# Causal attention scores by halves of 64 queries, in two 64-column tiles of TensorE

## The reference

```python
k = einsum('ihd,bpd->biph', W_K, x); q, v likewise
scores = einsum('biph,biqh->biqp', k, q)
masked = scores * tril - 1e10 * (1 - tril)
attn = softmax(masked / sqrt(128), axis=-1)
z = einsum('biqp,biph->biqh', attn, v)
out = einsum('df,bqf->bqd', W_O, z.reshape(b, q, 16 * 128))
```

## Time and profile before

| | |
|---|---|
| Runs: median (lowest to highest) of 3 | 977.67 us (977.49 to 978.47) |
| Profiled execution | 976.68 us |
| Its span, first to last instruction | 974.9 us |
| Mean granted TensorE clock | 0.995 of full |
| PE busy | 934.1 us, 96% |
| DVE, ACT, POOL busy | 627.8 us, 475.5 us, 239.0 us |
| DMA | 27.89 MB, mean 29 GB/s |

### The profile page before, as it was taken

The page is one execution under the profiler, slowest core; times in us unless marked ns, Lnnn a source line. Parts: engine busy times, 40 slices in busy tenths (PEclk is TensorE's granted clock), DMA queues, the critical chain, the costliest instruction groups (busy, mean ns, idle before and its releaser), DMA issues.

```text
span 974.9 us, 19976 instructions
## 1 busy us (share of the span) xinstructions
PE 934.1 (96%) x7621; PEld 793.7 (81%) x7621; DVE 627.8 (64%) x1383; ACT 475.5 (49%) x1593; POOL 239.0 (25%) x257
## 2 busy tenths in 40 slices
PE   7999999999999999999999999999999999999877
PEld 5777777899788888888888888888888887677657
DVE  6678887797875576564556454556456665777854
ACT  3877876444445554444344444434444554443431
POOL 3455786572011111111111010111111212110000
PEclk9999999999999999999999999999999999999989
DMA  8100000002330000000000000100010004000002
GB/s 304 38 2 3 2 2 2 2 1 90 108 152 1 1 1 2 1 1 2 1 1 2 1 1 1 44 18 1 1 58 30 1 1 176 1 2 2 2 1 87
DMA packets 10941, 27.89 MB, mean 29 GB/s; under 512 B 1824, under 2 KB 6976, under 8 KB 10208
## 3 DMA queue, kind: packets, MB, share of 16 engines
q1 hardware_dynamic: 10128, 26.41, 7.6%
q10 hardware_dynamic: 720, 0.20, 0.1%
HBM read 24.51 MB, written 2.10 MB: 27 GB/s over the span
## 4 chain that ended last, share of the span: by engine, by line
PE 84%; DVE 8%; ACT 4%; issue 2%; DMA 0%; POOL 0%; SPq 0%; DVEq 0%; ACTq 0%; POOLq 0%
PE bank L50 15%; PE bank L52 14%; PE bank L51 14%; PE bank L2035 6%; PE bank L1984 5%; PE bank L392 3%; PE bank L402 3%; PE bank L2025 3%; PE bank L1899 2%; PE bank L1908 2%; PE bank L414 2%; PE bank L1041 2%; PE bank L178 2%; PE bank L1031 2%; PE bank L1017 2%
## 5 line engine op out<-in xcount | busy, mean ns | idle before, releaser
L1845 POOL TENSOR_TENSOR wa_prob<-wa_prob,wa_rsum 128x512 f32<-128x512 f32 x64 | 67.5, 1055 | 405.2 <-DVE wa_rsum L2418 405.2
L2217 ACT ACTIVATE wa_prob<-wa_prob,wa_negmax 128x128 f32<-128x128 f32 x256 | 99.7, 390 | 66.3 <-DVE wa_negmax L2407 66.1
L50 PE MATMUL bank<-norm_xT_hi,wide_hi 128*128 128x512 f32 x256 | 106.0, 414 | 0.2 <-DVE norm_xT_lo L189 0.2
L51 PE MATMUL bank<-norm_xT_lo,wide_hi 128*128 128x512 f32 x256 | 101.0, 395 | 0.0
L52 PE MATMUL bank<-norm_xT_hi,wide_lo 128*128 128x512 f32 x256 | 101.0, 395 | 0.0
L2474 DVE TENSOR_TENSOR wa_z_lo<-bank,wa_z_hi 128x512 fp32r<-128x512 f32 x64 | 44.2, 691 | 86.9 <-ACT wa_z_hi L2251 86.4
L583 ACT ACTIVATE v_prob<-bank,la_negmax 128x128 f32<-128x128 f32 x256 | 91.1, 399 | 1.1 <-DVE la_negmax L661 1.1
L2225 ACT COPY wa_q<-bank 128x512 f32<-128x512 f32 x64 | 37.6, 587 | 93.6 <-PE bank L52 93.6
L2232 ACT COPY wa_v<-bank 128x512 f32<-128x512 f32 x64 | 37.3, 584 | 89.6 <-PE bank L52 89.6
L329 POOL TENSOR_TENSOR v_prob<-v_prob,la_rsum 128x512 f32<-128x512 f32 x64 | 66.5, 1041 | 51.8 <-DVE la_rsum L666 51.7
L173 POOL TENSOR_TENSOR norm_rstd<-norm_rstd,minus_half 128x4 f32<-128x4 f32 x23 | 24.6, 1069 | 206.1 <-DVE norm_rstd L133 175.2
(11 more groups left out here) (277 smaller groups left out, 2372.0 us busy)
## 6 DMA issues: line engine op xcount, KB each, us to landing
wide_raw<-in_wide_w SPq DMA_DIRECT2D x16, 512.0 KB, 6.8
em_w<-in_em_w SPq DMA_DIRECT2D x1, 4096.0 KB, 13.3
x<-in_x SPq DMA_DIRECT2D x4, 512.0 KB, 4.9
lc_kt<-in_ctx_rev SPq DMA_DIRECT2D x1, 2048.0 KB, 10.7
lc_toep<-in_toeplitz SPq DMA_DIRECT2D x1, 2048.0 KB, 14.5
li_kt<-in_ctx_rev SPq DMA_DIRECT2D x4, 512.0 KB, 6.6
out_x<-x SPq DMA_DIRECT2D x8, 256.0 KB, 2.9
w_or_y<-in_l_w SPq DMA_DIRECT2D x1, 1024.0 KB, 6.3
```

Source lines behind the costliest of these rows:

```text
L50: nc.tensor.matmul(out, a[0], b[0], start=start, stop=False, skip_group_check=True)
L51: nc.tensor.matmul(out, a[0], b[1], start=False, stop=False, skip_group_check=True)
L1845: nc.gpsimd.tensor_tensor(prob[:, s], prob[:, s], rsum[:, s, :].unsqueeze(2).to_broadcast([P, G, P]), ALU.mult).then_inc(prob_ok, 1)
L2217: last = nc.scalar.activation(prob[:, s, j, :], prob[:, s, j, :], ACT.Exp, bias=negmax[:, s, j:j + 1], scale=SCALE, accum_out=sums[:, s, j ...
```

## The change

Each batch's score matmul is replaced by two, each with 64 queries stationary. Their results go to partitions 0 to 63 (tile 0) and 64 to 127 (tile 1) of the bank. The first 64 queries take only the first 64 keys, except in steps 0 and 1, where they take all 128; the part that is then not written keeps finite scores of an earlier step, and the mask removes it. In even batches queries 0 to 63 are in tile 0, in odd ones in tile 1. For the odd batches the mask has its halves of rows exchanged, and the transposes of `turn` take a matrix with exchanged halves in place of the identity, which puts the queries back in order. The mask, the exchanged mask and the exchanged identity come in one load of 192 KB in place of 64 KB. The mask addition reads and writes the same elements as 2 x 256 in place of 4 x 128.

```diff
--- before.py
+++ after.py
@@ -1708,7 +1708,8 @@
         le_w, le_u = pr.le_w32, pr.le_u32
         v = sb("v", [P, 2, G, VH * HD])
         z = (sb("z_hi", [P, 2, GT], F32R), sb("z_lo", [P, 2, GT], F32R))
-        causal = sb("causal", [P, P])
+        masks = sb("masks", [P, 3, P])
+        causal, turned = masks[:, 0:2], (pr.ident, masks[:, 2])
         q = sb("q", [P, 2, GT])
         k = sb("k", [P, 2, GT])
         negmax = sb("negmax", [P, 2, G])
@@ -1812,7 +1813,7 @@
                 sp.dma_start(pr.wide_raw[hb][:, m], io["wide_w"][hb, :, m]).then_inc(w_in[hb], 16)
 
             sp.wait_ge(c_ps, 2 * CH)
-            sp.dma_start(causal[:], io["causal"]).then_inc(loaded, 16)
+            sp.dma_start(masks[:], io["masks"]).then_inc(loaded, 16)
             for m in (QW, KW, VW_, OW):
                 load_piece(0, m)
             sp.wait_ge(c_ps, 3 * CH)
@@ -1980,8 +1981,11 @@
                 pe.wait_ge(k_ok, BASE + n + 1)
                 pe.wait_ge(masked_ok, BASE + n - 1)
                 for j in range(G):
-                    t = slice(j * P, (j + 1) * P)
-                    last = nc.tensor.matmul(b_s[s][:, t], q[:, s, t], k[:, s, t], start=True, stop=True)
+                    for tile, late in enumerate((j % 2, 1 - j % 2)):
+                        rows, queries = [slice(at, at + P // 2) for at in (tile * P // 2, j * P + late * P // 2)]
+                        keys = slice(j * P, j * P + (P if late or n < 2 else P // 2))
+                        last = nc.tensor.matmul(b_s[s][rows, keys], q[:, s, queries], k[:, s, keys], start=True,
+                                                stop=True)
                 last.then_inc(s_ps, 1)
 
             def project_q(n, h_, v_before):
@@ -2022,7 +2026,7 @@
                 pe.wait_ge(prob_ok, BASE + n + 1)
                 pe.wait_ge(t_ok, BASE + n)
                 for j in range(G):
-                    last = nc.tensor.transpose(b_t[:, j * P:(j + 1) * P], prob[:, s, j, :], pr.ident[:])
+                    last = nc.tensor.transpose(b_t[:, j * P:(j + 1) * P], prob[:, s, j, :], turned[j % 2][:, :])
                 last.then_inc(t_ps, 1)
 
             def weigh(it, h_):
@@ -2399,9 +2403,10 @@
             def row_max(n, s, chain):
                 dve.wait_ge(s_ps, BASE + n + 1)
                 dve.wait_ge(t_ps, BASE + n - 1)
-                nc.vector.tensor_tensor(prob[:, s], b_s[s][:, :].rearrange("p (j k) -> p j k", j=G),
-                                        causal[:].unsqueeze(1).to_broadcast([P, G, P]), ALU.add)\
-                    .then_inc(masked_ok, 1)
+                nc.vector.tensor_tensor(prob[:, s].rearrange("p (i j) k -> p i (j k)", j=2),
+                                        b_s[s][:, :].rearrange("p (i n) -> p i n", i=2),
+                                        causal.rearrange("p j k -> p (j k)").unsqueeze(1)
+                                        .to_broadcast([P, 2, 2 * P]), ALU.add).then_inc(masked_ok, 1)
                 dve.wait_ge(masked_ok, BASE + n + 1)
                 chain.done(nc.vector.tensor_reduce(negmax[:, s, :], prob[:, s], AX, ALU.max))
                 nc.vector.tensor_scalar(negmax[:, s, :], negmax[:, s, :], -SCALE, None, ALU.mult)\
@@ -2675,7 +2680,9 @@
     wide = [w.reshape(P, DC, 4, 512).transpose(2, 0, 1, 3).reshape(4, P, -1) for w in wide[:3]] + \
         [wide[3].reshape(P, 4, -1).transpose(1, 0, 2)]
     r["wide_w"] = np.stack(wide, axis=2)
-    r["causal"] = np.triu(np.full((P, P), -1e30, np.float32), 1)
+    causal = np.triu(np.full((P, P), -1e30, np.float32), 1)
+    r["masks"] = np.stack([causal, np.roll(causal, P // 2, axis=0), np.roll(np.eye(P, dtype=np.float32), P // 2, axis=0)],
+                          axis=1)
 
     reverse = lambda t: t.reshape(DC, P, -1)[:, ::-1].transpose(1, 0, 2)
     r["li_w"] = np.stack([reverse(a["L1_xattn_Wk"].T), reverse(a["L1_xattn_Wv"].T), chunks(a["L1_xattn_Wq"].T),
```

## The result

The changed kernel takes 983.7 us (median of 5 runs, 983.43 to 987.09) against 977.64 us for the kernel before (median of 5, 975.94 to 978.47). The ratio is 1.0068, 95% interval 1.0054 to 1.0083: slower by 0.7%, some 6 us by the medians. The profiled execution's span grew from 974.9 to 981.7 us, 6.8 us.

A forecast was written before the change was run, and what follows sets the result against it. The prediction took PE to bound the kernel in the wide attention; +0.13 us in 62 heads and +0.33 in two gave +8.8 us, other parts 0. From the three-run median of 977.67 that made 986.5 us, range 982 to 995.

The forecast's parts named there:

- What bounds the kernel: Wide attention, 300 to 800 us: PE busy 497.49 of 500 us, so each nanosecond PE gains or loses is the kernel's.
- Tiles run side by side: Scores of a head: column tiles overlap, rounds 0.109 and 0.059 us; with switches and first loads 1.02 against 0.89 us.
- the seam's 0.34: Around each head's scores: two switches of 0.09 us and first loads of 0.05 and 0.11 come to 0.34 us.
- Heads 0 and 1 cost +0.33: Heads 0 and 1, with 128 keys throughout: scores take 1.22 us, +0.33 us each.
- Total 62 x 0.13 + 2 x 0.33 = +8.8 us: Scores of all 64 heads: +0.13 us in 62, +0.33 in two, +8.8 us in total, all on PE.
- Rival B: Scores: records start in program order across tiles, so long ones hold up short ones; +0.28 us a head, 995 us; 12%.
- The other parts: Transposes, mask addition and load of masks: 0 each; the load 2 us once if its cover fails.
- Rival A: Seams of each head's scores: changes of tiling stall nothing; 0.68 us a head, -13 us, 965 us; 5%.
- C: Scores: tiles in step, each round taking the longer one's time; +0.33 us a head, +21 us, 999 us; 7%.
- D: Scores: the halves don't overlap; +0.79 us a head, +51 us, 1029 us; 2%.
- E: Scores: a wash, terms at their low ends and the 64-column first load hidden; +0.02 us a head, 979.5 us; 5%.
- The rule of the Trainium skill: Scores: up to 2x where a dimension is at most 64; by that alone 0.67 us a head and 964 us.

The follow-up runs named there:

- the first experiment: Kernel before with one added 64-query by 64-key matmul a head, in a 64-column tile, ahead of the full score matmuls: 1003.58 us, ratio 1.0263.
- the third experiment: Changed kernel in two separate versions: all 128 keys for both halves of the queries, 995.05 us; odd batches not exchanged, 995.33 us.
- the early transposes: Changed kernel with transposes of heads 1 to 11 of each group moved right behind the scores: 988.39 us; without the places waiting for POOL: 982.01 us.
- the kernel with the tables alone: Kernel before with the 192 KB load, the 2 x 256 mask addition and every second transpose against a loaded matrix, scores not split: 977.22 us, ratio 1.0.
- Without the exchange: Changed kernel with early queries always in tile 0 and late ones always in tile 1: 995.33 us, ratio 1.0186.
- the fourth experiment: Changed kernel with tile 0's four score matmuls issued ahead of tile 1's four: 1007.36 us, ratio 1.0301.
- quarters: Kernel before with scores in four column tiles of 32 queries with 32, 64, 96 and 128 keys, rotated from batch to batch: 977.24 us, ratio 1.0.
- two heads in one visit: Kernel before with four 32-query tiles and two heads' scores back to back in five steps of each group: 972.38 us, ratio 0.9949.
- The same move in the kernel before: Kernel before with transposes of heads 1 to 11 of each group moved right behind the scores: 981.22 us, ratio 1.0052.

## Why the prediction was right

The direction, the mechanism and the range held: 983.7 us in 982 to 995, forecast 986.5; +6 to +7 us where the text has +8.8.

- *What bounds the kernel:* held. PE's busy time grew by 7.4 us and the span by 6.8, but PE's wait at the ends of groups took up a part (below).
- *Tiles run side by side, seam 0.09 to 0.10, first loads 0.05 and 0.11, rounds 0.109 and 0.059:* held as a sum. 1.02 us and L50's own 0.23 make 1.25; the chain has 0.82 + 0.43 = 1.25. The kernel before is 1.13 by the same reading, so the head's price is +0.12 and not +0.13; by the starts of the score records it is 0.114 in the mean of the heads that grew in full. That a seam costs what was said is shown by the first experiment, the rounds by the third. How the seam's 0.34 divides into stalls and loads rests on the rows of before; the early transposes bear out one part of it, with some 0.04 us where 0.05 to 0.06 was expected.
- *Heads 0 and 1 cost +0.33:* held. Worked out from the starts of the score records in both traces, their steps grew by 0.32 and 0.34 us.
- *"Total 62 x 0.13 + 2 x 0.33 = +8.8 us, all on PE":* this step was mis-sized. Of the 63 intervals from one head's first score record to the next, seven did not grow (by 0.02 us or less) and three grew by only 0.06 to 0.07. Nine of the ten lie at the ends of the groups, one inside the last group. In the chain of the kernel before:

```profile
517.15 0.91 PE bank L2035 x8
...
524.10 1.16 PE bank L2035 x8
```

Between these two rows the chain leaves PE for ACT and DVE; that head's scores, at 517.88 in the timeline, lie beside it. The distance is 6.95 us, and in the changed kernel, from 520.72 to 527.67, it is 6.95 us again. The row of the mask addition in the chain could have told this: where DVE is on the path, PE's scores aren't. The argument of the prediction, idle time of 0.0 ahead of L1984 and L2025 and so no wait that can take up a difference, looked at two groups and left out a third, the weighing. What PE waits for from 280 to 810 us, before and after:

```profile
PE bank L2035 <- DVE wa_probT L2461: 2.5, 5, 0.6
...
PE bank L2039 <- DVE wa_probT L2466: 2.0, 5, 0.5
```

Four of the five waits are 0.11 to 0.12 us shorter after the change, and these are four of the seven steps that didn't grow; at the other three a wait of 0.07 us is gone, which leaves 0.05 of each open. The 63 intervals grew by 6.7 us in all. Against the forecast 1.1 us are missing at the ten places, 0.8 in the size of the other heads (0.114 where the sum has 0.13) and 0.1 at the last head, whose way out lies behind the last interval.
- *Two sums of the prediction are a little off.* 62 x 0.13 + 2 x 0.33 is 8.7 as printed; 8.8 comes from 0.132. Rival B's +18 gives 995.7 and not 995, so the range up to 995 doesn't quite take it in. Neither changes what the measurement says.
- *The other parts cost nothing:* shown within 1 us, by the kernel with the tables alone.
- *Rival A* (free seams) is refuted by the first experiment, *B* by the changed kernel's own 0.82 (it asked for 0.97), *C* by the third experiment, *D* by the chain. *E* by the head's +0.12 (it asked for +0.02). The rule of the Trainium skill, "TensorEngine Tiling (Array Packing)", section Theoretical Speedup, would have given 964; the overlap it speaks of is there, and the seams decide.
- The Trainium skill's "TensorE: Matmul & The Clock Gate", section The mechanism, on which rival B drew, has matmuls start and end in program order; across two tiles this case's traces don't agree. Without the exchange the fourth matmul of tile 0 starts 0.40 us behind the first record, and the third of tile 1, which stands before it in the program, at 0.50, in all of the 62 heads. The order in the program matters all the same, as the fourth experiment shows.

## What to carry to other kernels

A change of PE's tiling has a fixed price, here about 0.34 us for going into column tiles and back out, of which the groups of busy time show next to nothing; read it from the distance of starts where tilings meet. How it divides into stalls and loads that aren't hidden is an estimate. Split a matmul into column tiles only if the rounds save more than that, which here took quarters and two heads in one visit; balance the tiles, and alternate them in the program. And count only the places at which the engine is on the chain: a head beside another engine's chain costs nothing. Look for them by the waits of all of the engine's groups, not only of those that are changed.

## What the runs showed of the hardware that was not expected

- Tiles with unequal matmuls run apart: two tiles with two long and two short ones each, in opposite order, take the sum of one tile (0.82 us with the way in). A tile with short matmuls alone gets ahead of the other, out of program order (0.40 against 0.50 us, as above). But they aren't two unlimited queues: issued tile by tile the second tile starts 0.39 us late, and the scores take 1.20 us.
- Waits of 1.94 us on PE, inside a stage that is otherwise full, were each followed by a fall of the granted clock (0.65 over one stretch of 4 us, 0.92 over the next), with steps of 0.42 us where 0.23 is usual. The same happened at waits of 2.04 us with quarters. The same move in the kernel before had waits of 1.86 us, and its clock stayed at 1.00. The waits differ little and what surrounds them differs too, so what decides stays open.
- A PE transpose in fp32 takes a matrix with rotated rows in place of the identity at the same speed (mean records of 272 ns, and 275 with the identity), so that a permutation of queries costs nothing where a transpose follows anyway.
